# Softmax sums of both halves made once a pair, inverted once and spread by transfers

## The reference

```python
q, k, v = map(to_heads, (q, k, v))
q = apply_rotary(q, cos, sin) * DHEAD ** (-0.5)
k = apply_rotary(k, cos, sin)
kt = jnp.einsum('bhnd,hde->bhne', k, W_bilinear)
sim = jnp.einsum('bhid,bhjd->bhij', q, kt)
attn = jax.nn.softmax(sim, axis=-1)
out = jnp.einsum('bhij,bhjd->bhid', attn, v)
```

## Time and profile before

| | us |
|---|---|
| median of 3 runs | 3682.24 |
| the profiled execution | 3680.91 |
| its span | 3679.1 |
| TensorE busy | 3552.7 (97%) |
| VectorE busy | 3004.0 (82%) |
| GpSimd busy | 2786.8 (76%) |
| ScalarE busy | 1719.3 (47%) |

### The profile page before, as it was taken

One profiled execution on the slowest core, in us unless ns is written; L12 is line 12 of the kernel. 1 busy time (PEld: TensorE's weight loads), 2 busy tenths in 40 slices (PEclk: granted clock), 3 DMA queues, 4 the chain that ended last, 5 costly groups with the idle time before them and its releaser, 6 DMA issues. The chain is left out here.

```text
span 3679.1 us, 69836 instructions
## 1 busy us (share of the span) xinstructions
PE 3552.7 (97%) x22106; PEld 2307.7 (63%) x22106; DVE 3004.0 (82%) x4377; ACT 1719.3 (47%) x3196; POOL 2786.8 (76%) x1407
## 2 busy tenths in 40 slices
PE   6999999999999999999999999999999997899999
PEld 4666556555655555665565556556666663788888
DVE  6788888888888788888888888888877777799998
ACT  2444444444444444444444444444444443455555
POOL 2888888888888888888888888889888886122222
PEclk7999999999999999999999999999999998899999
DMA  4112111121112111211121112111211002333332
GB/s 179 59 59 80 63 53 51 61 81 54 59 61 81 57 61 61 78 61 62 59 81 62 60 56 79 61 61 59 76 53 53 36 36 67 90 95 100 96 94 72
DMA packets 200227, 254.52 MB, mean 69 GB/s; under 512 B 17760, under 2 KB 141152, under 8 KB 195424
## 3 DMA queue, kind: packets, MB, share of 16 engines
q1 hardware_dynamic: 190688, 242.16, 19.3%
q10 hardware_dynamic: 9216, 8.39, 0.6%
HBM read 119.41 MB, written 61.08 MB: 49 GB/s over the span
## 5 line engine op out<-in xcount | busy, mean ns | idle before, releaser
L398 POOL TENSOR_TENSOR prob_sum<-prob_sum,prob 128x1024 f32<-128x1024 f32 x762 | 1883.6, 2472 | 310.8 <-ACT prob L461 270.6
L461 ACT ACTIVATE prob<-scores 128x512 f32<-128x512 f32 x2048 | 1087.1, 598 | 918.7 <-PE scores L674 888.4
L599 DVE TENSOR_REDUCE row_max<-max_scores 128x1 f32<-128x512 f32 x1536 | 1010.2, 686 | 328.8 <-PE max_scores L713 310.1
L839 PE MATMUL attn_out<-prob,v 128*64 128x512 f32 x4096 | 932.6, 597 | 0.0
L662 PE MATMUL scores<-q_hi,k_hi 64*128 64x512 f32 x2048 | 823.0, 404 | 1.7 <-issue 1.7
L674 PE MATMUL scores<-neg_max,ones_rows 64*128 64x512 f32 x2048 | 795.6, 389 | 0.1
L666 PE MATMUL scores<-q_hi,k_lo 64*128 64x512 f32 x2048 | 795.6, 390 | 0.0
L670 PE MATMUL scores<-q_lo,k_hi 64*128 64x512 f32 x2048 | 795.5, 389 | 0.0
L839 PEld LDWEIGHTS attn_out<-prob,v 128*64 128x64 f32 x4096 | 286.0, 137 | 559.5 <-issue 558.2
L713 PE MATMUL max_scores<-k_hi,q_hi 64*128 64x512 f32 x1536 | 548.4, 410 | 9.3 <-DVE k_lo L640 3.0
L662 PEld LDWEIGHTS scores<-q_hi,k_hi 64*128 64x128 f32 x2048 | 375.5, 184 | 255.4 <-issue 207.8
(11 more groups left out here) (134 smaller groups left out, 5015.3 us busy)
## 6 DMA issues: line engine op xcount, KB each, us to landing
rows<-rows SPq DMA_DIRECT2D x512, 128.0 KB, 2.0
w_group<-w_parts SPq DMA_DIRECT2D x30, 1536.0 KB, 6.8
attn_normalised<-z_stage SPq DMA_DIRECT2D x128, 256.0 KB, 2.0
v<-attn_normalised SPq DMA_DIRECT2D x64, 512.0 KB, 4.1
x_turned_parts<-x_tile_parts SPq DMA_DIRECT2D x49, 256.0 KB, 2.7
xt_batch<-x_turned_parts SPq DMA_DIRECT2D x7, 1792.0 KB, 10.4
x_in<-in_x SPq DMA_DIRECT2D x64, 128.0 KB, 3.8
out_y<-result ACTq DMA_DIRECT2D x64, 128.0 KB, 1.7
```

The source lines that it names most:

```text
L398: nc.gpsimd.tensor_tensor(psums[half][:, :, :], a, prob[:, n % RING, :, :], ALU.add).then_inc(added, 1)
L461: nc.scalar.activation(prob[:, n % RING, e, :], S[e][n % 2][:, :], ACT.Exp).then_inc(exped[e], 1)
L599: nc.vector.reduce_max(mx[1 - u][:, e, n // 2, n % 2:n % 2 + 1], bank_of(e, jj)[:, :], axis=AX.X)\
L839: nc.tensor.matmul(O[rows(e), :], V[k // 2 % 2][:, j, col:col + DH], prob[:, n % RING, e, :], start=j == 0, stop=j == 7).then_inc(pv_made[ ...
```

## The change

The sums of half 0 are no longer made in quad 2. All four sums of a pair (two halves, two heads) are made in quad 0 of the next pair as four products of 32 columns, each into its own 32 partitions of `shared`. VectorE inverts the bank once. Eight transfers of 32 rows copy each inverted row group to twice its partitions in a new tile `inv_rows`. GpSimd multiplies both halves in quad 1, after its adds of tiles 6 and 7, and SyncE stores both after the swap of the queries. There are three buffers of `prob_sum` in turn instead of two. The diff, cut:

```diff
-        psums = [sb(f"prob_sum{h}", [P, 2, HALF], F) for h in two]
+        psums = [sb(f"prob_sum{s}", [P, 2, HALF], F) for s in range(3)]
+        inv_rows = sb("sum_inverted_rows", [P, 2, HALF], F)
...
+            def spread(t):
+                wait(sp, z_made, 2 * t)
+                at_rest()
+                wait(sp, inv_made, t + 1)
+                at_rest()
+                for h in two:
+                    for e in two:
+                        for r in two:
+                            row = e * DH + r * GRAIN
+                            sp.dma_start(inv_rows[row:row + GRAIN, h, :], inv[(2 * h + e) * GRAIN:(2 * h + e + 1) * GRAIN, :])\
+                                .then_inc(inv_in, 16)
...
                 if k >= 1:
-                    store_z(t - 1, 1)
+                    spread(t - 1)
...
                     for c in two:
                         swap(Q, t, c)
+                if k >= 1:
+                    for h in two:
+                        store_z(t - 1, h)
+                if proj:
                     p = (k + 2) % PAIRS
...
-                if attn:
-                    store_z(t, 0)
...
             def norm_z(t, h):
-                wait(pool, inv_made, 2 * t + h + 1)
+                wait(pool, inv_in, 128 * (t + 1))
...
-                        if jj == 0 and q == 1 and k >= 1:
-                            norm_z(t - 1, 1)
-                        if jj == 0 and q == 3 and attn:
-                            norm_z(t, 0)
+                        if q == 1 and jj > 1 and k >= 1:
+                            norm_z(t - 1, jj - 2)
                         if proj and q in (1, 2) and jj == 2:
                             rope(t, q - 1)
...
-            def invert(t, h):
-                wait(dve, l_made, 4 * t + 2 * h + 2)
-                wait(dve, z_made, 2 * t + h)
+            def invert(t):
+                wait(dve, l_made, 4 * t + 4)
+                wait(dve, inv_in, 128 * t)
                 nc.vector.reciprocal(inv[:, :], M[:, :]).then_inc(inv_made, 1)
...
-            def sums(t, h, last=False):
...
+            def sums(k, t):
+                if k == T - 1:
+                    pe.wait_ge(added_last, 7)
+                    wait(pe, added, 14 * t + 7)
+                else:
+                    wait(pe, added, 14 * t + 14)
+                for h in two:
+                    for e in two:
+                        row = (2 * h + e) * GRAIN
+                        nc.tensor.matmul(M[row:row + GRAIN, :], ones[:, 0:GRAIN], psums[(2 * k + h) % 3][:, e, :], start=True, stop=True,
+                                         tile_position=(0, row)).then_inc(l_made, 1)
```

More of the change, by code:

```diff
@@ L158 @@
 RING = 8
+GRAIN = 32
 MAX = 4
@@ L221, in attention @@
         negm_made, nm_turned, nm_hi, nm_lo, nm_in = (sem(x) for x in ("neg_max_made", "max_turned", "max_hi", "max_lo", "max_in"))
-        l_made, inv_made, z_copied, z_made = (sem(x) for x in ("sums_made", "sums_inverted", "z_copied", "z_made"))
+        l_made, inv_made, inv_in, z_copied, z_made = (sem(x) for x in ("sums_made", "sums_inverted", "inverted_in", "z_copied", "z_made"))
         z_stored = [sem(f"z_stored{h}") for h in two]
@@ L265, in _ @@
         def _(sp):
-            for s in swap_in[K] + swap_in[Q] + z_stored + [nm_in, x_in] + x_stored:
+            for s in swap_in[K] + swap_in[Q] + z_stored + [nm_in, inv_in, x_in] + x_stored:
                 sp.sem_inc(s, CREDIT)
@@ L366, in _ @@
             pairs(sp, span)
-            store_z(T - 1, 1)
+            spread(T - 1)
+            for h in two:
+                store_z(T - 1, h)
             for h in two:
@@ L387, in add @@
                 half, j = n // 8, n % 8
+                total = psums[(2 * k + half) % 3][:, :, :]
                 if j == 0 or (k == T - 1 and half):
@@ L392, in add @@
                 if j == 1:
-                    wait(pool, l_made, 4 * (t - 1) + 2 * half + 2)
+                    wait(pool, l_made, 4 * (t - 1) + 4 * half)
                     a = prob[:, (n - 1) % RING, :, :]
@@ L396, in add @@
                     wait(pool, added, 14 * t + adds_by(n - 1))
-                    a = psums[half][:, :, :]
-                nc.gpsimd.tensor_tensor(psums[half][:, :, :], a, prob[:, n % RING, :, :], ALU.add).then_inc(added, 1)
+                    a = total
+                nc.gpsimd.tensor_tensor(total, a, prob[:, n % RING, :, :], ALU.add).then_inc(added, 1)
             def rope(t, x):
@@ L427, in _ @@
             pairs(pool, span)
-            norm_z(T - 1, 1)
+            for h in two:
+                norm_z(T - 1, h)
         @blk.scalar
@@ L554, in add_last @@
                     wait(dve, exped[e], 16 * (T - 1) + n + 1)
-                a = prob[:, 0, :, :] if n == 9 else psums[1][:, :, :]
+                total = psums[(2 * T - 1) % 3][:, :, :]
+                a = prob[:, 0, :, :] if n == 9 else total
                 if n == 9:
-                    wait(dve, l_made, 4 * (T - 2) + 4)
+                    wait(dve, l_made, 4 * (T - 1))
                 else:
                     dve.wait_ge(added_last, n - 9)
-                nc.vector.tensor_tensor(psums[1][:, :, :], a, prob[:, n % RING, :, :], ALU.add).then_inc(added_last, 1)
+                nc.vector.tensor_tensor(total, a, prob[:, n % RING, :, :], ALU.add).then_inc(added_last, 1)
             def row_sums():
@@ L645, in _ @@
             pairs(dve, span)
-            invert(T - 1, 1)
+            invert(T - 1)
         @blk.tensor
@@ L695, in max_score @@
                     if q == 1 and i == 2:
-                        wait(pe, inv_made, 2 * (t - 1) + 2)
-                    if q == 3 and i == 2:
-                        wait(pe, inv_made, 2 * t + 1)
+                        wait(pe, inv_made, t)
                 elif q and i == 0:
@@ L817, in span @@
                                     wait(pe, x_red[1], 16 * (t + 1) + 2)
[L818 to L827, removed]
+                                wait(pe, inv_made, t - 1)
+                            sums(k - 1, t - 1)
                         half = q // 2
@@ L841, in _ @@
             pairs(pe, span)
-            wait(pe, inv_made, 2 * (T - 1) + 1)
-            sums(T - 1, 1, True)
+            wait(pe, inv_made, T - 1)
+            sums(T - 1, T - 1)
 def feed_forward(nc, x, z_scr, kept, alpha, g1, b1, g2, b2, bias2, ident_in, out):
```

7 lines of the change are left out of this document (2 added, 5 removed).

## The result

The changed kernel takes 3876.26 us (median of 4 runs, 3871.99 to 3880.33) against 3682.06 us before: a ratio of 1.0528 (95% interval 1.051 to 1.0547). The forecast was 3871 us. The profiled execution took 3871.99 us, with a span of 3870.1 us and a mean granted clock of 0.968, where it was 0.988 before.

What follows compares the result with a forecast made beforehand. TensorE, busy 97% of the span, was taken to bound the kernel. Waits 163 - block saved 57 + width change 11 + clock 72 = 189 us, added to 3680.9: 3870, as a median 3871 us; range 3795 to 3930.

Steps and rivals of the forecast that it cites:

- Its main step: Quad 2: ScalarE's copy of half 0 waits for the store until about 1019.45 instead of 1016.08, delaying tile 10.
- The size of the wait: TensorE before tile 10: a wait of 2.5 us in each pair, with ends of 1.5 and 3.3 us.
- The chain: GpSimd's multiplication ends at 1017.14, SyncE stores at 1017.40, it lands at 1019.40, then copy, exponentials, and tile 10 at 1020.6.
- The waits: TensorE: 133 us in pairs 1 to 53, 15 in 54 to 61, 6 in 62, 2 in 63; 163 with the end's 7.
- the vanished 4.67: Pair 63: the earlier 4.67 us wait for the sums of its half 0 goes, against a copy late by about 7.
- The product block: Sums on TensorE: four 32-column products run at once in 0.90 us, so quad 2's block is saved, 57 us.
- change of width: Behind the new block on TensorE: products start only at its end, 0.18 us later a pair, 11 us in all.
- the rate worked out from the Trainium skill: Block of sums: four column tiles would take a quarter longer than one, making the sum some 15 us longer.
- The clock: TensorE's clock falls behind three in four of 53 waits and three in ten of 8, 1.7 us each: 72 us.
- The rule of the Trainium skill: TensorE's clock: only longer idle gaps lower it, so this term is 0; rival 1, 3799 us, chance 0.17.
- The end: At attention's end, the spreading and a second multiplication stand ahead of the last store: +7 us (6 to 8).

Runs made afterwards that it cites:

- four buffers: The changed kernel with two buffers of `z_stage` for each half, used by even and odd pairs in turn: 3602.89 us, 0.9789 of the kernel before.
- moving the store alone: The kernel before with only the store of half 0 moved, behind the next pair's swap of the queries: 3794.4 us, ratio 1.031.
- the move of the multiplication alone: The changed kernel with GpSimd's two multiplications one place earlier, behind the adds of tiles 5 and 6: 3877.66 us.

## Why the prediction was right

**The mechanism.** Its main step, that the store of half 0 now holds up ScalarE's copy and with it tile 10, is shown by four buffers (the wait goes, and 273 us with it) and by moving the store alone (113 us). The size of the wait was right: 2.5 us forecast, 2.57 us idle and 2.7 us of delay measured in the pair shown. That the total came within 5 us of the forecast is luck, as the terms below show.

**One link was wrong, and it did not matter to the sum.** The chain ended in GpSimd's multiplication at 1017.14 with the swap already out at 1016.36. The sum took the adds to "stand beside the same VectorE work as before". They don't: they now begin just ahead of VectorE's `q_lo`, the instruction before the rotation that the swap waits for.

```profile
1113.64 3.09 DVE L628 TENSOR_TENSOR q_lo<-rows,q_hi 128x1024 fp32r<-128x1024 f32 x1
```

It takes 3007 ns on average here; before, where GpSimd's short multiplication ran at its start in 56 of the 64 pairs, it took 1881 ns. In all 64 pairs here it ends 1.08 us after the instruction of GpSimd that runs at its start, an add in 63 of them. So the multiplication ends at 1016.7 and the swap at 1017.2. The two nearly equal links changed places; the move of the multiplication alone, the remedy that the prediction's chain suggests, gives nothing.

**The waits, term by term.** Forecast 133 + 15 + 6 + 2 = 156 us for pairs 1 to 63. Measured 184.6 us. Of the 28 us, 13 are pairs 1 to 53 (146 us; the median is 2.6 us, and in the ten pairs over 3.1 the store lands or goes out later than usual), 5 are pairs 54 to 61 (20 us; the wait shrank to 2.3 us, not 1.9), 6 are pair 62, which waits 12.2 us instead of 6, and 5 are only a way of counting: pair 63 is idle for 6.8 us, less the vanished 4.67 us the forecast 2. Each wait also costs some 0.3 us above its idle time: laid over the kernel with four buffers, instruction by instruction, TensorE's restarts take 203 us more besides the clock, where the idle time is 184.6 us. That was left out; the first record behind a wait takes 0.49 us instead of 0.39, and what the rest is was not looked into.

**The product block.** 57 us less 11 were forecast for one block saved and one change of width. Measured are 0.99 us for four against 0.90 for two, 0.09 us x 63 = 6 us more, and the block of quad 2 is gone, 59 us by laying TensorE's starts over each other (besides the 4.67 us wait of the earlier trace rows): 53 us instead of 46. Any cost of the change of width is within those 6 us, for the products behind the block begin 0.99 us after its start, before its last record ends at 1.06 us. The Trainium skill ("TensorEngine Tiling (Array Packing)", Tiling Modes) has 128x32 as four tiles, and the trace agrees; the rate worked out from the Trainium skill ("TensorE: Matmul & The Clock Gate", Part 3), four a quarter longer than one, is above what was measured, 0.99 us against the 0.86 us of one product, 15%.

**The transposes.** The missed term. Their wait, 35 us, goes and so does what else VectorE's late result costs there: by TensorE's starts these stretches take 44 us less than before. The misses of the sum cancel: 43 us too little for the waits of the loop (203 less the vanished 4.67, instead of 156) and 8 for the clock; on the other side these 44 and 7 of the product block. 3871 and 3876 lie so near each other by this offset.

**The clock.** Forecast 72 us against the kernel before, measured 80 us. Here the judgement was right in its parts: three in four of pairs 1 to 53 were to have a fall, and 40 of 53 have one; of the eight pairs behind them three in ten, and 2 of 8 have one; together 75 us. The rest comes mostly from the long waits of pairs 62 and 63, which the forecast left out. The rule of the Trainium skill ("TensorE: Matmul & The Clock Gate", HAM oscillation), by which only longer gaps than the usual ones here would bring the clock down, disagrees with this, and the measurement decides. Nor is the answer a yes or no: of two waits of 2.3 us one had a fall and the other none, and the share with a fall grows with the length.

**The end.** The step before the feed-forward stage cost what was forecast: the wait of `up_bank` is 24.8 us in the kernel with four buffers and was 17.2 us before, 7.6 us more.

**The sum.** From the kernel with four buffers to the changed one: 184.6 us of waits + 77 us of clock = 262 of 273 us, and what the 63 restarts cost above their idle time is the rest.

## What to carry to other kernels

A store that only has to be done "some time before the buffer is used again" is free while it is early, and its slack is a number to be kept: here it was over 20 us, and one reordering spent it and 3.6 us more. When work is batched so that it comes later, look for the buffer whose release moves with it, and give it a second one first; the gain (79 us) was there all along. Where two links of a chain end within half a microsecond of each other, no remedy for one of them alone can be judged by its price alone, and since many of the waits of 1.8 us and more cost clock here as well as their own time, a stall of TensorE is to be priced with both.

## What was not expected of the hardware

- Whether TensorE's clock falls behind a wait is a matter of odds that grow with its length: none of 118 waits up to 1.75 us, 17 of 43 at 2.0, 60 of 89 at 2.6, all of 25 over 3.2 us. A fall costs 1.7 us.
- VectorE's `x_tile_normed` (128 x 256) takes 0.47 us with nothing beside it, and up to 2.72 us beside an instruction of GpSimd: it ends 0.28 us after that one does. Its mean went from 2.6 to 1.4 us by another neighbour, and to 0.8 us by a later start beside the same one. VectorE's `q_lo` (128 x 1024) ends 1.08 us after GpSimd's add in the same way; that other VectorE instructions do so is not said by this.
- Four fp32 products of 32 columns and 512 rows take 0.99 us together, two of 64 columns 0.90 us, one of 128 columns 0.86 us.
- Eight issues of transfers of 32 rows took SyncE 5.0 us in the loop by the median (4.9 to 6.5), 0.63 us each, where one store of 128 rows takes 0.36 us.
